# Cross-attention and FFN on one core: row-tile loads and weight looks issued behind P's transposing DMA

## The reference, cut to what matters

```
x = x + attention(layernorm(x), ctx, ctx, w_q, w_k, w_v, w_out, mask)   # 32 heads, 8 key/value groups, head size 32
x = x + ffn(layernorm(x), w12, b12, w3, b3)                            # silu(x1) * x2 between the two products
attention: scores = q k^T / sqrt(32); where(mask, scores, min); softmax; weights times v; then times w_out^T
```

## Time and profile before

| what | us |
|---|---|
| median of 3 runs | 1066.66 |
| the profiled execution's own time | 1065.12 |
| its span (first to last instruction) | 1063.3 |
| TensorE busy in the span | 1024.2 |
| DVE / GpSimd / ScalarE busy | 685.4 / 492.4 / 429.9 |
| TensorE idle before `weigh`'s L1402, released by P's transposing DMA | 7.2 in 4 waits |

### The profile page before, as it was taken

How to read it: one execution, slowest core, us unless ns; L and a number is a source line. 1 busy time by engine, 2 the same in 40 slices (tenths; PEclk the granted TensorE clock), 3 DMA queues, 4 the chain that set the end, 5 groups by cost and what they waited for, 6 DMA issues and landing times.

```text
span 1063.3 us, 21836 instructions
## 1 busy us (share of the span) xinstructions
PE 1024.2 (96%) x8400; PEld 697.8 (66%) x8400; DVE 685.4 (64%) x2092; ACT 429.9 (40%) x967; POOL 492.4 (46%) x456
## 2 busy tenths in 40 slices
PE   7888799999999999999999999999999999999998
PEld 6777666867778677786655544444444788468853
DVE  6889888777777777688856422836865356625431
ACT  6756455645546455465475420113441112301110
POOL 2769801624626246267797689127852301212000
PEclk9998899999999999999999999999999999999999
DMA  9658598897898888679785634395659741884201
GB/s 366 231 145 185 124 259 198 210 245 209 250 210 227 228 209 199 142 196 227 184 250 107 172 158 156 102 301 214 240 185 213 252 120 41 209 243 123 80 30 50
DMA packets 230775, 199.11 MB, mean 187 GB/s; under 512 B 177040, under 2 KB 187280, under 8 KB 225808
## 3 DMA queue, kind: packets, MB, share of 16 engines
q1 hardware_dynamic: 230672, 197.72, 67.9%
HBM read 119.04 MB, written 35.65 MB: 145 GB/s over the span
## 4 chain that ended last, share of the span: by engine, by line
PE 76%; DVE 10%; DMA 3%; POOL 2%; issue 2%; ACT 1%; SPq 1%; DVEq 0%; POOLq 0%; ACTq 0%
PE bank_dense L1327 46%; PE bank_spare L1327 11%; PE bank_score L1472 6%; PE bank_spare L1472 5%; DVE arena_attn L1797 3%; PE bank_av L1472 3%; DMA arena_attn<-arena_attn 2%; PE bank_score L1384 1%; DVE arena_in L1636 1%; POOL arena_in L870 1%; DVE arena_attn L1807 1%; POOL arena_in L866 1%; PE bank_av L1402 1%; DVE arena_rows L1691 1%; PE bank_av L1406 1%
## 5 line engine op out<-in xcount | busy, mean ns | idle before, releaser
L1142 ACT ACTIVATE arena_attn<-arena_attn,arena_in 128x128 f32<-128x128 f32 x512 | 162.8, 392 | 126.7 <-DVE arena_in L1797 126.4
L925 POOL TENSOR_TENSOR arena_attn<-arena_attn 128x512 f16<-128x512 f32 x85 | 99.0, 1181 | 156.5 <-ACT arena_attn L1149 156.5
L1327 PE MATMUL bank_dense<-arena_attn,arena_rows 128*128 128x512 f16 x768 | 166.4, 379 | 0.0
L1327 PE MATMUL bank_dense<-arena_rows,arena_in 128*128 128x256 f16 (+1 forms) x1104 | 152.0, 295 | 3.0 <-issue 1.4
L1797 DVE CUSTOM_DVE_ANT_0 arena_attn<-bank_score,arena_in 128x128 f32<-128x128 f32 x512 | 143.5, 346 | 0.4 <-POOL arena_attn L925 0.3
L1327 PEld LDWEIGHTS bank_dense<-arena_attn,arena_rows 128*128 128x128 f16 x768 | 75.1, 98 | 90.2
L1327 PEld LDWEIGHTS bank_dense<-arena_rows,arena_in 128*128 128x128 f16 x1104 | 107.5, 98 | 38.4 <-issue 1.7
L1327 PE MATMUL bank_dense<-arena_out,arena_attn 128*128 128x512 f16 x576 | 127.8, 379 | 0.0
L1327 PE MATMUL bank_spare<-arena_rows,arena_in 128*128 128x256 f16 (+1 forms) x816 | 112.3, 295 | 3.1 <-DVE arena_rows L1761 3.1
L1327 PEld LDWEIGHTS bank_spare<-arena_rows,arena_in 128*128 128x128 f16 x816 | 78.7, 98 | 29.6 <-DVE arena_rows L1761 4.1
L1327 PEld LDWEIGHTS bank_dense<-arena_out,arena_attn 128*128 128x128 f16 x576 | 55.6, 98 | 63.3
(11 more groups left out here) (217 smaller groups left out, 1867.3 us busy)
## 6 DMA issues: line engine op xcount, KB each, us to landing
arena_rows<-x SPq DMA_DIRECT2D x32, 512.0 KB, 5.9
arena_in<-w_scratch SPq DMA_DIRECT2D x64, 256.0 KB, 3.0
arena_attn<-q_scratch SPq DMA_DIRECT2D x48, 256.0 KB, 4.6
arena_rows<-w_t SPq DMA_DIRECT2D x12, 1024.0 KB, 6.2
arena_rows<-ctx_t SPq DMA_DIRECT2D x8, 1024.0 KB, 5.8
q_scratch<-arena_attn SPq DMA_DIRECT2D x16, 512.0 KB, 5.4
x_scratch<-arena_rows SPq DMA_DIRECT2D x16, 512.0 KB, 3.9
arena_out<-x_scratch SPq DMA_DIRECT2D x16, 512.0 KB, 6.0
```

The source lines that it names most:

```text
L925: ins = pool.tensor_tensor(p_split[:, g % 2, u, 1], e[:, g % 2, u], p_split[:, g % 2, u, 0], ALU.subtract)
L1142: ins = act.activation(head, head, ACT.Exp, bias=neg_max[:, g % 2, h:h + 1], scale=-1.0)
L1327: ins = pe.matmul(dst, lhs(a, c), rhs(b, c), start=(c == chunks[0] and n == 0), stop=(c == chunks[-1] and n == 2))
```

## The change

Three things on SP and one on DVE. (1) `load_tile` moves from the head of steps 0 and 1 behind `turn_prob` and behind `stack_k` (step 0) or `stack_q` (step 1). (2) The first look of a block moves from step 0 to step 1, behind that step's `load_tile`, and its maximum on DVE from step 2 to step 3. (3) The w3 look stays in step 3 but is issued behind `load_x_res`; since the maximum before it is now taken in step 3 too, its wait is for that one.

```diff
-LOOK_AT = {2: "w{0}", 4: "w3{2}", 6: "w{1}"}
+LOOK_AT = {3: "w{0}", 4: "w3{2}", 6: "w{1}"}
...
                     g = GROUPS * a + s
-                    if t < NB - 1 and s in (0, 1):
-                        load_tile(2 * t + 2 + s)
                     if t < NB and s in (2, 7):
                         spill_q(t, int(s == 7))
...
                     if s == 1:
                         stack_q(a, 1)
+                    if t < NB - 1 and s in (0, 1):
+                        load_tile(2 * t + 2 + s)
                     if t < NB and s == 4:
                         stack_q(t, 0)
                     if t < NB - 1 and s == 3:
                         load_ctx(t + 1)
-                    if 2 <= t < 6 and s == 0:
-                        load_look(look_at(t, 2), w12_t[2 * (t - 2)])
-                    if 2 <= t < 6 and s == 3:
-                        load_look(look_at(t, 4), w3_t[t - 2])
+                    if 2 <= t < 6 and s == 1:
+                        load_look(look_at(t, 3), w12_t[2 * (t - 2)])
                     if 2 <= t < 6 and s == 5:
                         load_look(look_at(t, 6), w12_t[2 * (t - 2) + 1])
                     if t >= 2 and s == 3:
                         load_x_res(t - 2, 1)
+                    if 2 <= t < 6 and s == 3:
+                        load_look(look_at(t, 4), w3_t[t - 2])
```

## The result

The change makes the kernel slower: 1073.63 us (median of 9 runs, 1069.94 to 1083.3) against 1066.66 (9 runs, 1064.38 to 1073.94), ratio 1.0079 with a 95% interval of 1.0056 to 1.0102. 1070.0 was forecast, that is +3.4 us; the ratio makes it +8.4. Two later comparisons of the same two kernels gave 1.0085 [1.0063, 1.0108] and 1.0051 [1.003, 1.0072], so 5.4 to 9 us. The profiled execution took 1075.03 us, 9.9 more than the profiled one of before.

The account below looks back on a forecast made before the run. TensorE, 1024.2 us busy of a 1063.3 us span, was taken as the bound. Terms 1.4 + 1.0 + 0 + 0.2 + 0.8 = 3.4 on a 1066.66 median gave 1070.0 us; own range 1067.5 to 1072.5, whole range 1062.5 to 1074.5.

Parts of the forecast that it names:

- the w3 look decides: Rival, chance 0.15: look 4 us late for DVE, spread_top 1.3 us later in each of four blocks, 5 for 0.8: 1074.3 us.
- SP's queue around P: SP's DMAs act as one line; each transfer pays its time to every P behind it.
- More than 8 us: Sign that the forecast is right: P(9)'s issue holds SP for more than 8 us.
- A tile's price, 1.4 us each: In SP's line, a row tile ahead of a P delays it by 1.4 us, bounds 0 and 2.0.
- The rival drawn from it: Faster rival, chance 0.20: queued transfers overlap more, P(9) and P(17) land in time, 4.0 us go: 1062.7 us.
- Block 1, +1.4: load_tile(5), now ahead of P(1), adds its 1.4 us to weigh(1)'s stall; bounds 0 and +2.0.
- a wait that stays at 1.8 us: Sign at weigh(1) in block 1: an unchanged wait puts the tile's price at nothing.
- Block 2, +1.0: weigh(8)'s 2.51 us stall goes, weigh(9) waits 3.5 us for P(9); net +1.0, bounds -2.5 and +1.6.
- Block 3, 0: P(16)'s 1.48 us stall goes, weigh(17) waits for P(17) to 220.45; net 0, bounds -1.5 and +0.5.
- the w3 look, +0.8: Behind load_x_res in step 3, DVE waits 2.5 us, mostly absorbed; +0.8 over four blocks, bounds 0 and +5.
- the 3.5 that the prediction itself had set: Lateness in us of the w3 look for DVE from which the rival "the w3 look decides" holds.
- Blocks 4 to 6, +0.2: No waits for P to win there; P(25) and P(33) get 1.5 MB more ahead of them: +0.2 in all.

Follow-up runs that it names:

- the exchange of two DMAs: w3 look issued ahead of load_x_res in step 3: in the changed kernel 1068.48 us, 1.0026 to before; in the kernel with only the looks moved 1062.64 us, 0.997.
- the looks alone: Kernel before with only the looks and the first look's maximum moved as in the change, row tiles left at the head of steps 0 and 1: 1066.4 us, 1.0005.
- The same exchange on the kernel before: Kernel before with one swap alone, load_x_res ahead of the w3 look in step 3: 1066.32 us, 1.0003.
- second profile of the change: The unaltered change run once more against the kernel before: 1073.66 us, 1.0085; its profiled execution had a span of 1068.1 us.
- the filled change: The change plus ten identity transposes each before weigh(9) and before spread_top in step 7 of blocks 2 to 5: 1071.64 us, 1.0046; again 1071.3, 1.0041.
- tiles alone: Kernel before with only the two load_tile calls of a block moved behind turn_prob and stack_k or stack_q: 1071.45 us, 1.0051.
- looks with the w3 look first: Kernel before with the looks moved, tiles not, and the w3 look kept ahead of load_x_res: 1062.64 us, 0.997.
- the filled kernels: Change, and kernel before, each with ten transposes before weigh(9) and before spread_top in blocks 2 to 5: change 1071.64 and 1071.3 us, before 1067.03 us, 1.0006.
- with blocks 3 and 4 filled: The change with transposes before spread_top in blocks 3 and 4 and weigh(9): 20 each, plus 32 before weigh(1), 1074.41 us, 1.0082; ten each, none before weigh(1), 1074.58, 1.0084.
- block 1's tiles back: The change with block 1's row tiles at the head of their steps again, other tiles and looks still moved: 1071.92 us, 1.0064 to before.

## Why the prediction was wrong

The sign was right, the size under half. How SP's queue moves the waits for P was right in the main; the step on the w3 look was not. The measured 1073.63 us lie outside the forecast's own 1067.5 to 1072.5, and nearest to the third rival, "the w3 look decides", with 1074.3 us and a chance of 0.15. By the prediction's own steps, in the profiled run:

**SP's queue around P.** Right in kind. P(9) was issued at 144.46 and held SP for 8.82 us behind tile 7 and the 1 MB look:

```profile
142.54 0.43 SPq L587 DMA_DIRECT2D arena_rows<-x  x1
143.01 0.43 SPq L719 DMA_DIRECT2D arena_rows<-w_t  x1
...
144.46 8.82 SPq L695 DMA_TRANSPOSE arena_attn<-arena_attn  x1
```

More than 8 us had been named as the sign. It landed 10.9 us after its issue, at 155.34, and weigh(9) waited.

**A tile's price, 1.4 us each.** Too high for P(9) and P(17). From the start of its block (120.40 before, 123.42 after, by the table) P(9) landed at 31.92 us where it had been 31.59, 0.3 later and not 1.4. P(17) landed at 28.1 where it had been 28.8. P(16) had landed at 16.1 us in the block in place of 21.2, so the queue behind it, tile and look among it, started that much sooner, and that can have hidden most of the tile's time; no run separates it. (Two readings of the prediction were loose here: the 4.8 us of "P alone" are the median of all 64, whatever was ahead of them, and 1.46 us a tile would have made the sum 0.1 higher, 0.06 in each of blocks 1 and 2, and not 0.2.) The Trainium skill ("DMA: Bandwidth & Descriptors", Two DMAs through the same engine are not ordered) has descriptors start in order and be pipelined. The rival drawn from it failed on the sign, but here its rule fits P(9) and P(17) better than a full price for each tile. The transposing DMA itself did not overlap so: SP was held by P(9) to 153.28 us, and the look issued ahead of it had landed at 151.6.

**Block 1, +1.4.** About right. Measured +1.9 over the block in this execution: the wait grew from 1.81 to 4.38, and later steps gave part of it back. Over all profiles the moved tile puts the start of weigh(1) off by 0.7 to 3.0 us. The sign that the prediction had named, a wait that stays at 1.8 us, misleads: two profiles of the change have 1.6 us there, with a later weigh(1) all the same.

**Block 2, +1.0.** The waits went as predicted, weigh(8)'s out and weigh(9)'s in, and netted 0.0: weigh(9) began 31.97 us into the block and had begun at 32.02. Nearly all of the 1.4 us that the block lost is step 4, which took 10.36 for 9.07 at the lower clock. A right sum for a wrong reason.

**Block 3, 0, and the w3 look, +0.8: the step that failed.** The term for the look took DVE's demand from block 3 of before, with the stall before weigh(16) in it, and used that one block for all four. The prediction had the look land at 230.6 and DVE want it at 228.1, 2.5 us apart. In times from the start of block 3 (190.22 before, 194.65 after, the table's lines added up) the landing was foreseen well: 40.4 forecast, 40.1 measured. But the demand was 1.6 us earlier: 37.9 forecast, 36.3 measured, since DVE began to wait at 234.78 - 3.80 = 230.98. The prediction removed weigh(16)'s stall and put it all back before weigh(17) through the tile's price. That price was not paid, weigh(17) came 1.6 us earlier in the block (28.70 for 30.34), and the gain ran straight into DVE's wait for the look. With 3.8 us of lateness block 3 was past the 3.5 that the prediction itself had set for its third rival. Even that bound was too high: looks 1.6 to 1.9 us late left step 7's wait as it was (block 5, three profiles of the change), and looks 2.2 to 3.8 us late made it 0.5 to 1.8 us longer (blocks 3 and 4 of the same profiles).

In block 4 the prediction missed something else. Its rows had no stall there and hence no later demand, and the look had 0.1 us to spare. The prediction weighed P(25)'s delay only as a wait of TensorE, and not that SP, held by it, issues the look 2.2 us later. So the look was 3.19 us late there.

The waits of step 7 then grew by 1.82 us in each of blocks 3 and 4 (that rival had said 1.3 in each of four), and the lower clock, for which the prediction had no term, put 4.6 on top. 0.8 had been allowed; the steps 7 lost 8.3, of which 1.6 had been gained earlier in block 3. In the two later profiles of the change, block 4 lost 1.4 and 0.6, so the size varies between executions with how far a wait grows.

That the late look is the cause of the loss in steps 7 is shown by the exchange of two DMAs, worth 0.53% in the change (0.25 to 0.59% against its three measurements) and 0.35% in the looks alone. The same exchange on the kernel before, 0.03%, shows that it costs only together with the other moves; that this is the removed stall in block 3 rests on the demand times, and that it is SP's delay behind P(25) in block 4 on the one pair of traces.

**Blocks 4 to 6, +0.2.** P(25) and P(33) were hardly waited for in this run: 0. In the second profile of the change weigh(25) waited 0.74 us, and in the filled change block 4 has a step 3 of 10.3 us, so the margin is thin. What P(25) did by way of SP and the look is told above.

**The sum.** By the ratios of medians the pieces nearly add: tiles alone +0.51%, looks with the w3 look first -0.30%, together +0.26% measured against +0.21; the w3 look behind the residual +0.53%. How much of the loss in the whole is the lower clock stays open between nothing and about half (4.6 of 9.9 us in the profiled run, 2.0 us by the medians of the filled kernels, with intervals that overlap).

## What to carry to other kernels

A stall that is taken away moves forward every demand behind it: before counting a stall as saved, lay the landing times of the next steps' transfers against demands that are earlier by that stall. Here the 1.5 us saved at weigh(16) made up a third of the step from a look 1.0 us early to one 3.8 late; the exchange and a fuller queue did the rest. The issuing engine counts as well: what holds it puts off everything issued behind, as in block 4. Check each block by its own times; block 4 had 0.1 us to spare where block 3 had 1.0. Where two loads are issued together, the one whose consumer comes first and has followers goes first. And a new wait of TensorE like the 2.5 and 2.7 us here should carry a price for the clock as well, with a range, since it comes in some executions and not in others, and the 2.51 us before weigh(8) had left the clock full.

## What the hardware showed that was not expected

**Waits and clock.** In step 7 of blocks 3 and 4, idle times of 0.88 and 0.70 us left the clock full, and those of 2.70 and 2.52 us had products at half clock behind them. The length alone does not decide. The second profile of the change has the lower clock (0.86 over the step) behind 1.64 us in step 7 of block 3, and before, 2.51 us ahead of weigh(8) left it at 1.00. Ten small transposes in such a wait went with a clock of 1.00 in one execution and of 0.87 over the step in another, each time with 1.61 us of idle time left. The Trainium skill ("TensorE: Matmul & The Clock Gate", HAM oscillation) describes DMA waits between bursts of products that bring the lower clock each time; the traces agree in kind, 0.50 behind an idle time of 2.70 us (a wait for DVE here), but it did not come each time.

**The same order, other waits.** Filling some steps moved the lower clock to others: with blocks 3 and 4 filled it showed in blocks 2 and 5 in the profiles of both such kernels, where the unaltered change had none. It is not the fill alone: with block 1's tiles back and nothing filled, step 7 of block 5 took 14.52 us. Why the late look falls on other blocks in other executions is not explained.
